# Attention loop of a polynomial-attention and expert block: units of two heads, fp32 scores, value products two key blocks behind, another reciprocal, the mask on the first square

## The chip, the cores and the metric

The kernel runs on one core of one Trainium2 chip. The metric is device time in microseconds of one execution, the median of several runs. Smaller is better.

The engines are named as in the profile: PE is TensorE (PEld its weight loads), DVE is VectorE, ACT is ScalarE, POOL is GpSimd, SP is the engine that issues DMAs.

## The reference

```python
x = L0_attn_x                                    # (4, 512, 512): 4 batches, 512 tokens, 512 features
x = x + attention(_layernorm(x))                 # 16 heads of 32
x = x + moe(_layernorm(x))                       # 16 experts, 4 per token, and a shared expert

# attention, for each batch and head
q, k, v = split(x @ w_qkv)                       # rotary position on q and k
q = layernorm_32(q) * ln_scale + ln_bias         # over the 32 features of a head; k the same
a = tril((q @ k.T) ** 4)                         # causal, fourth power instead of exp
out = (a / a.sum(-1)) @ v                        # then heads side by side, @ w_out
```

The expert part (router scores, choice of four experts, gate, up and down products) is the same before and after.

## The kernel before

One program of hand-written engine queues with semaphores. Its first part handles the four batches one after the other: `sequence(0, None)` is unrolled, batches 1 to 3 are a loop over the same body. The second part handles 96 tiles of 128 tokens through the shared expert and the chosen experts; the change does not touch it.

A batch has these stages:

1. **qkv, four blocks of 128 tokens.** PE multiplies (line 462), DVE applies the rotation and the norm of each head (lines 1159 to 1183), with one square on ACT between (line 746, released by line 1173, waited for by line 1177). PE transposes q and k (line 473), and ACT writes them with scale and bias: once as fp16 (line 712, the high half) and once as fp32 (line 716). DVE subtracts the two (`split_qk`, line 1149) and so gets the fp16 low half. The subtraction of block m-1 stands between lines 1173 and 1177 of block m.
2. **The attention loop.** Its 16 steps i are 4 groups of 4 heads (g) times 4 key blocks of 128 tokens (kb = i % 4). Because of the causal mask a step works on 512, 384, 256 and 128 query columns for kb 0 to 3, keys on the partitions. For each step PE makes the scores of 4 heads into 4 PSUM banks, each as three fp16 products (high-high, high-low, low-high; line 538). ACT squares each head from PSUM into `s_sq` (line 770). The second square goes into `s_p4`: heads 0 and 2 on DVE (line 1193), heads 1 and 3 on ACT (line 762). POOL multiplies the first 128 columns of each of the 4 heads by the causal mask (line 853). PE then makes the value product and, with a matrix of ones, the denominators (line 552), both accumulated over the key blocks of the group in banks 6 and 7. These products run one step behind the scores. `s_sq` has one buffer, `s_p4` has two, so the second square of step i waits for the products of step i-2.
3. **The end of a group.** `finish` on DVE takes the reciprocal of all 128x512 denominators (line 1141; a head's denominator stands on its 32 partitions alike) and multiplies (line 1143). The first value product of the next group (kb = 0) waits for it, since it starts banks 6 and 7 anew. `finish` of group g stands on DVE's queue after the second squares of step 4g+4, and for the last group after the loop.
4. **Beside the loop.** In every step ACT splits a piece of the expert weights into fp16 high part and rest (lines 682 and 684), and POOL makes the low part (line 861, `split_lo`), which is queued on POOL between the masks of one step and the next. In batches 1 to 3 DVE also does the routing of the batch before, a piece after the squares of most steps (`group_sums` in step 1 to `place_rows` in steps 9 to 12), and in all batches the statistics of the next batch's first norm in step 12 and its norm in step 14, which ACT follows with line 726.
5. **Output projection** (line 566), residual (line 1224), second norm, transposes.

The order on each engine is the order written in its function; nothing reorders it.

## Time and profile before

| | us |
|---|---|
| median of 3 runs (1252.7 to 1258.45) | 1253.88 |
| profiled execution, first to last instruction | 1278.8 |
| attention loop, batch 0 | 79 |
| attention loop, each of batches 1 to 3 | 95 |
| qkv stage of batch 1, with the transposes for the router | 54 |
| expert part, from 680 us on | 599 |

The profiled execution is known by its span alone; it is 24.9 us longer than the median of the runs without a profile. A row of the timeline has the start in us, the length in us (of one instruction, or from the first start to the last end of several), engine, line, operation, what is written and read, shape, and in brackets how long the engine had been idle and what ended that. A granted clock of 1.00 is TensorE at 2.4 GHz, 0.50 at 1.2 GHz.

### The profile page before, as it was taken

The numbers are of one execution on the slowest core, as the hardware profiler recorded it, in microseconds if no ns is written. First come the engines' busy times: TensorE is split into PE (matmuls) and PEld (weight loads), VectorE is DVE, ScalarE is ACT, GpSimd is POOL, SyncE is SP. The second block draws the span as 40 slices with busy tenths as digits, with TensorE's granted clock in tenths as the row PEclk, the third lists the DMA queues.
The fourth block names the chain that finished last, engine by engine and source line by source line (L and its number), as shares of the span: only waits on it lengthen the run. The fifth ranks groups of instructions, "written<-read, shape, count | busy, mean of one in ns | idle before, by whom it ended". The sixth has DMA issues, their size and how long they took to land. (4 is left out here: it accounts for less than half of the span.)

```text
span 1278.8 us, 21813 instructions
## 1 busy us (share of the span) xinstructions
PE 1013.0 (79%) x5786; PEld 483.4 (38%) x5787; DVE 782.5 (61%) x1641; ACT 571.1 (45%) x1018; POOL 503.3 (39%) x738
## 2 busy tenths in 40 slices
PE   5956799666997669976588889888888888878893
PEld 2422245222444214442145445344344344434341
DVE  2855578587695885858955866444544545544442
ACT  2377624767147672366735324333333333323330
POOL 0047500556003751026631102555555555555552
PEclk9977898677996689967787889999999999989997
DMA  8015430144501438104445786777877778877774
GB/s 323 1 50 188 159 131 1 50 149 146 183 3 49 140 107 327 69 0 148 148 149 178 264 321 216 188 171 178 187 185 179 170 177 191 192 154 183 169 178 77
DMA packets 76782, 194.36 MB, mean 152 GB/s; under 512 B 9920, under 2 KB 11072, under 8 KB 75328
## 3 DMA queue, kind: packets, MB, share of 16 engines
q1 hardware_dynamic: 58816, 150.58, 34.5%
q0 software_dynamic: 17920, 43.26, 18.9%
q8 instruction: 17, 0.28, 0.1%
q14 instruction: 29, 0.24, 0.1%
HBM read 132.72 MB, written 61.10 MB: 152 GB/s over the span
## 5 line engine op out<-in xcount | busy, mean ns | idle before, releaser
L606 PE MATMUL bank<-arena,xgT 128*128 (+1 forms) x1152 | 287.4, 387 | 4.0 <-ACT xgT L817 3.1
L853 POOL TENSOR_TENSOR s_p<-s_p,c_causal 128x128 f32<-128x128 f32 x256 | 128.8, 530 | 400.0 <-DVE s_p L1193 397.6
L552 PE MATMUL bank<-s_p,vtok 128*32 128x128 f32 (+3 forms) x512 | 118.0, 605 | 95.9 <-DVE arena L1143 49.5
L810 ACT ACTIVATE hT<-bank 128x512 f16<-128x512 f16 x96 | 57.3, 597 | 276.5 <-PE bank L616 264.6
L462 PE MATMUL bank<-arena 128*128 128x512 f32 x384 | 168.6, 597 | 2.0 <-issue 2.0
L606 PEld LDWEIGHTS bank<-arena,xgT 128*128 128x128 f16 x1152 | 109.6, 100 | 133.5 <-issue 44.4
L627 PE MATMUL bank<-wd,hT 128*128 128x512 f16 x576 | 152.7, 405 | 0.7 <-ACT hT L810 0.7
L898 POOL DMA_INDIRECT out<-yy,sidx x80 | 128.4, 1605 | 45.7 <-issue 44.7
L861 POOL TENSOR_TENSOR arena<-arena 128x768 f16<-128x768 f32 x68 | 115.7, 1702 | 71.9 <-ACT arena L684 71.5
L817 ACT ACTIVATE xgT<-bank 128x1024 f16<-128x1024 f16 x96 | 98.2, 1023 | 90.7 <-PE bank L597 89.1
L1367 DVE TENSOR_SCALAR yy<-bank,hsc 128x512 f32<-128x512 f32 x80 | 60.0, 750 | 125.8 <-DMA out<-yy,sidx 106.6
L1193 DVE TENSOR_TENSOR s_p<-arena 128x512 f32<-128x512 f32 (+3 forms) x128 | 82.8, 679 | 78.0 <-ACT arena L770 73.3
L770 ACT ACTIVATE arena<-bank 128x512 f32<-128x512 f32 (+3 forms) x256 | 97.8, 436 | 63.9 <-PE bank L538 37.4
L597 PE MATMUL bank<-ident,xg 128*128 128x128 f16 x768 | 62.7, 228 | 74.7 <-DMA xg<-xn_scratch,gidx 74.7
L462 PEld LDWEIGHTS bank<-arena 128*128 128x128 f32 x384 | 72.6, 192 | 89.9 <-issue 89.9
L892 POOL DMA_INDIRECT xg<-xn_scratch,gidx x80 | 85.0, 1063 | 41.3 <-issue 40.3
L1327 DVE TENSOR_TENSOR hh<-sg,bank 128x256 f32<-128x256 f32 x96 | 40.3, 419 | 90.3 <-ACT sg L826 85.7
L597 PEld LDWEIGHTS bank<-ident,xg 128*128 128x128 f16 x768 | 49.1, 102 | 112.4 <-DMA xg<-xn_scratch,gidx 103.4
L552 PEld LDWEIGHTS bank<-s_p,vtok 128*32 128x32 f32 x512 | 28.5, 121 | 153.3 <-POOL s_p L853 94.7
L552 PE MATMUL bank<-s_p,ones 128*32 128x128 f32 (+3 forms) x512 | 85.6, 578 | 0.0
L538 PE MATMUL bank<-arena 32*128 32x512 f16 (+3 forms) x768 | 61.5, 363 | 23.1 <-ACT arena L770 11.8
L627 PEld LDWEIGHTS bank<-wd,hT 128*128 128x128 f16 x576 | 55.4, 103 | 53.2 <-issue 11.3
(155 smaller groups left out, 1453.3 us busy)
## 6 DMA issues: line engine op xcount, KB each, us to landing
wd<-w_scratch SPq DMA_DIRECT2D x82, 512.0 KB
arena<-w_experts SPq DMA_DIRECT2D x34, 768.0 KB, 5.9
w_scratch<-arena SPq DMA_DIRECT2D x34, 768.0 KB, 4.5
arena<-w_scratch SPq DMA_DIRECT2D x17, 1024.0 KB, 8.0
xin<-x SPq DMA_DIRECT2D x5, 1024.0 KB, 9.1
arena<-x SPq DMA_DIRECT2D x4, 1024.0 KB, 7.1
x_scratch<-arena SPq DMA_DIRECT2D x4, 1024.0 KB, 4.5
xn_scratch<-vtok SPq DMA_DIRECT2D x4, 1024.0 KB, 5.0
```

Of the source, the lines that this page charges most:

```text
L462: mm = pe.matmul(bank[w][:], xnT[:, c, m * P:m * P + P], wqkv[:, c, w * E:w * E + E], start=(c == 0), stop=(c == EC - 1))
L552: mm = pe.matmul(bank[6 + n][r, P * kb:N], w, s_p4[:, (i - 1) % 2, j, 0:N - P * kb], start=(kb == 0), stop=(kb == MB - 1), skip_group_chec ...
L597: mm = pe.transpose(oct16(bank[k])[:, c], xg[:, k, 0:E].bitcast(F16)[:, c * P:c * P + P], ident16[:])
L606: mm = pe.matmul(bank[2 + k][:], xgT[:, k, xh * EC + c, :], w, start=(c == 0 and xh + wh == 0), stop=(c == EC - 1 and xh == 1))
L627: mm = pe.matmul(bank[5 + k][:], hT[:, k, hh_ * FC + c, :], wd[:, k, wh, c, :], start=(c == 0 and hh_ + wh == 0), stop=(c == FC - 1 and hh ...
L770: act.activation(s_sq[:, j, 0:N - P * kb], bank[j][:, 0:N - P * kb], ACT.Square, scale=1.0 / (QS * QS)).then_inc(sq_done, 1)
L817: act.activation(xgT[:, k], oct16(bank[k]), ACT.Copy).then_inc(gT_sb, 1)
L853: pool.tensor_tensor(d, d, C["causal"][:], ALU.mult).then_inc(p4_masked, 1)
L861: pool.tensor_tensor(halves[:, j, 1, a], stage[:, j, a], halves[:, j, 0, a], ALU.subtract).then_inc(lo_done, 1)
L892: pool.indirect_dma_start(out=xg[:, k], out_offset=None, in_=xn_dram, in_offset=bass.IndirectOffsetOnAxis(ap=gidx[:, k:k + 1], axis=0)).th ...
L898: pool.indirect_dma_start(out=out, out_offset=bass.IndirectOffsetOnAxis(ap=sidx[:, k:k + 1], axis=0), in_=yy[:, k], in_offset=None, comput ...
L1193: dve.tensor_tensor(s_p4[:, i % 2, j, 0:N - P * kb], s2, s2, ALU.mult).then_inc(p4_done[0], 1)
```

## The change

- q and k are written once, as fp32 (`qT`, `kT`); the fp16 halves, the factor of 64 and `split_qk` go. The scores of a head are one fp32 product in place of three fp16 products.
- A step has two units u of two heads each. ACT squares a unit in one instruction of 2 x w columns, from two PSUM banks. POOL masks the first 128 columns of both heads in one instruction, now in `s_sq`, between the two squares. DVE makes the second square of all units, one instruction each; ACT makes none.
- PE's value products run two steps behind the scores (`LAG = 2`).
- `finish` transposes the denominators in blocks of 32x32, takes the reciprocal of 16 columns in place of 512, and transposes them back, spread over 32 columns. It now stands after the squares of step 4g+5.

```diff
@@ PE
-                pe.wait_ge(qk_lo, b * (2 * MB) + 2 * MB)
+                pe.wait_ge(qkT_sb, b * (2 * MB) + 2 * MB)
-                for i in range(NG * MB + 1):
+                for i in range(UNITS // 2 + LAG):
...
-                        order = [(n, j) for n in range(3) for j in range(HG)]
-                        for n, j in order:
-                            if i and n == 0:
-                                pe.wait_ge(sq_done, b * (NG * MB * HG) + (HG * (i - 1) + j + 1))
...
-                            mm = pe.matmul(bank[j][:, 0:N - P * kb], k16[r, kh, g, P * kb:P * kb + P],
-                                           q16[r, qh, g, P * kb:N], start=(n == 0), stop=(n == 2))
+                        for u in (2 * i, 2 * i + 1):
+                            if u >= 2:
+                                pe.wait_ge(sq_done, b * UNITS + (u - 1))
...
+                            for j in (u % 2 * 2, u % 2 * 2 + 1):
+                                r = slice(D * j, D * j + D)
+                                mm = pe.matmul(bank[j][:, 0:N - P * kb], kT[r, g, P * kb:P * kb + P],
+                                               qT[r, g, P * kb:N], start=True, stop=True)
+                            mm.then_inc(scores_ps, 1)
...
+                                if n == 0 and j % 2 == 0:
+                                    pe.wait_ge(p4_done, b * UNITS + (2 * (i - LAG) + j // 2 + 1))
@@ ACT
+                for i in range(UNITS // 2):
                     w = N - P * (i % MB)
+                    for u in (2 * i, 2 * i + 1):
+                        j = u % 2 * 2
+                        act.wait_ge(scores_ps, b * UNITS + (u + 1))
+                        if u >= 2:
+                            act.wait_ge(p4_done, b * UNITS + (u - 1))
+                        act.activation(s_sq[:, j:j + 2, 0:w], wide(j)[:, :, 0:w], ACT.Square).then_inc(sq_done, 1)
@@ POOL
+                        pool.wait_ge(sq_done, b * UNITS + (u + 1))
+                        d = s_sq[:, j:j + 2, 0:P]
+                        pool.tensor_tensor(d, d, C["causal"][:].unsqueeze(1).to_broadcast([P, 2, P]),
+                                           ALU.mult).then_inc(sq_masked, 1)
@@ DVE
             def finish(b, g):
                 dve.wait_ge(pv_done, b * (NG * MB) + (g * MB + MB))
-                dve.reciprocal(rec, bank[7][:])
+                blocks = lambda a: a.rearrange("p (c i) -> p c i", i=D)
+                dve.transpose(den_t, bank[7][:])
+                dve.drain()
+                dve.reciprocal(inv[:], blocks(den_t)[:, :, 0])
+                dve.drain()
+                dve.transpose(blocks(rec), inv[:].unsqueeze(2).to_broadcast([P, N // D, D]))
                 dve.drain()
                 dve.tensor_tensor(attT[:, g, :], bank[6][:], rec, ALU.mult).then_inc(att_done, 1)
...
                     if i >= 2:
+                        dve.wait_ge(pv_done, b * (UNITS // 2) + (i - 1))
+                    for u in (2 * i, 2 * i + 1):
+                        j = u % 2 * 2
+                        dve.wait_ge(sq_masked, b * UNITS + (u + 1))
+                        s2 = s_sq[:, j:j + 2, 0:N - P * kb]
+                        dve.tensor_tensor(s_p4[:, i % 2, j:j + 2, 0:N - P * kb], s2, s2, ALU.mult).then_inc(p4_done, 1)
-                    if i and kb == 0:
+                    if i > MB and kb == 1:
                         finish(b, i // MB - 1)
```

## Rows read from the trace of the kernel before

**Rows 1.** The page's busy times, shares of the span and instruction counts.
```profile
PE 1013.0 (79%) x5786; PEld 483.4 (38%) x5787; DVE 782.5 (61%) x1641; ACT 571.1 (45%) x1018; POOL 503.3 (39%) x738
```
**Rows 2.** Stretches of time: length, busy time by engine, granted clock, DMA.
```profile
76.00:155.00 79.00, 57.76 (x455) 18.29 (x456) 46.37 (x51) 62.88 (x133) 57.83 (x80) 0.79 0.44 148
229.00:324.00 95.00, 64.67 (x506) 23.94 (x507) 72.15 (x130) 66.38 (x136) 58.85 (x80) 0.75 0.37 124
```
**Rows 3.** Timeline, batch 1, step 3 to 4, POOL and DVE.
```profile
248.93 4.17 POOL L853 TENSOR_TENSOR s_p<-s_p,c_causal 128x128 f32<-128x128 f32 x4 [1.31 <-DVE s_p L1193]
248.97 1.49 DVE L999 TENSOR_TENSOR rb<-mb 128x1024 f32<-128x1024 f32 x1
```
**Rows 4.** Timeline, batch 0, second group: the end of a group, until the next.
```profile
96.40 3.34 DVE L1141 RECIPROCAL qkn<-bank 128x512 f32<-128x512 f32 x1
99.82 0.69 DVE L1143 TENSOR_TENSOR arena<-bank,qkn 128x512 f32<-128x512 f32 x1
100.56 1.94 PE L552 MATMUL bank<-s_p,vtok 128*32 128x512 f32 x8 [4.50 <-DVE arena L1143]
114.72 3.35 DVE L1141 RECIPROCAL qkn<-bank 128x512 f32<-128x512 f32 x1
```
**Rows 5.** Stretches of the same: the stall of PE, and the products after it.
```profile
96.40:100.50 4.10, 0.00 (x0) 0.00 (x0) 4.03 (x4) 4.04 (x9) 3.23 (x5) 0.86 0.82 256
100.50:104.10 3.60, 3.54 (x16) 0.60 (x16) 0.94 (x3) 1.18 (x2) 3.04 (x5) 0.50 0.35 145
```
**Rows 6.** Timeline, batch 1: qkv stage, the square on ACT and what stands beside it.
```profile
193.61 1.28 DVE L1149 TENSOR_TENSOR arena<-s_p,arena 128x512 f16<-128x512 f32 x2
193.72 1.06 ACT L746 ACTIVATE arena<-arena 128x1024 f32<-128x1024 f32 x1 [1.16 <-DVE arena L1173]
```
**Rows 7.** Groups by line and shape: count, busy us, mean ns of one, idle before.
```profile
L716 ACT ACTIVATE s_p<-bank,ln_b,ln_s 128x512 f32<-128x512 f32 x32 | 25.1, 783 | 0.0
L817 ACT ACTIVATE xgT<-bank 128x1024 f16<-128x1024 f16 x96 | 98.2, 1023 | 90.7 <-PE bank L597 89.1
L770 ACT ACTIVATE arena<-bank 128x512 f32<-128x512 f32 x64 | 34.9, 599 | 26.9 <-PE bank L538 18.0 <-DVE s_p L1193 8.8
L770 ACT ACTIVATE arena<-bank 128x256 f32<-128x256 f32 x64 | 21.2, 385 | 26.6 <-DVE s_p L1193 13.6 <-PE bank L538 12.6
L684 ACT ACTIVATE arena<-arena 128x768 f32<-128x768 f32 x68 | 57.3, 843 | 2.1
L853 POOL TENSOR_TENSOR s_p<-s_p,c_causal 128x128 f32<-128x128 f32 x256 | 128.8, 530 | 400.0 <-DVE s_p L1193 397.6 <-ACT s_p L762 2.2
L1166 DVE TENSOR_TENSOR arena<-arena 128x1024 f32<-128x1024 f32 x16 | 19.6, 1225 | 1.5
L1179 DVE RECIPROCAL hs<-hs 128x32 f32<-128x32 f32 x16 | 5.6, 353 | 6.2 <-ACT hs L748 6.2
```
**Rows 8.** Timeline, batch 0 and 1: second squares, a mask, a low part.
```profile
78.32 0.69 DVE L1193 TENSOR_TENSOR s_p<-arena 128x512 f32<-128x512 f32 x1 [2.18 <-ACT arena L770]
79.17 0.45 POOL L853 TENSOR_TENSOR s_p<-s_p,c_causal 128x128 f32<-128x128 f32 x1 [76.47 <-DVE s_p L1193]
82.61 1.64 POOL L861 TENSOR_TENSOR arena<-arena 128x768 f16<-128x768 f32 x1 [1.15 <-ACT arena L684]
93.48 3.00 DVE L1193 TENSOR_TENSOR s_p<-arena 128x512 f32<-128x512 f32 x2 [1.15 <-ACT arena L770]
299.31 1.28 DVE L1193 TENSOR_TENSOR s_p<-arena 128x512 f32<-128x512 f32 x2
```
**Rows 9.** Timeline, scores of 512 columns, batch 0 and batch 1.
```profile
76.20 1.47 PE L538 MATMUL bank<-arena 32*128 32x512 f16 x12 [2.75 <-DVE arena L1149]
247.05 0.82 PE L538 MATMUL bank<-arena 32*128 32x512 f16 x12
```
**Rows 10.** Timeline, DVE, batch 1: the stretch with routing, and the end.
```profile
276.70 0.69 DVE L1193 TENSOR_TENSOR s_p<-arena 128x512 f32<-128x512 f32 x1 [3.66 <-ACT arena L770]
319.88 3.36 DVE L1141 RECIPROCAL qkn<-bank 128x512 f32<-128x512 f32 x1 [2.29 <-PE bank L552]
```

More of the change, by code:

```diff
@@ L61 @@
 CH = NCOL // P
+UNITS = NG * MB * 2
+LAG = 2
 NEG = 1.0e30
@@ L161, in build @@
         xnT = over([EC, N])
-        q16, k16 = (over([NG, N]).bitcast(F16).rearrange("p g (h n) -> p h g n", h=2) for _ in range(2))
+        qT, kT = (over([NG, N]) for _ in range(2))
         s_sq = over([HG, N])
@@ L206, in build @@
         hs = sa("hs", [P, 3, 2 * H])
[L207 removed]
+        den_t, rec = qkn[:, 0:N], qkn[:, N:2 * N]
+        inv = sa("inv", [P, N // D])
         xn16 = vtok[:].rearrange("p m e -> p (m e)").bitcast(F16).rearrange("p (m h e) -> p m h e", m=MB, h=2)
```

81 lines of the change are left out of this document (19 added, 62 removed).

## The prediction

> **What bounds the kernel now.** I read the page first, then the table of stretches, then the timeline engine by engine, and last the groups by line. No engine fills the span: PE is busy for 79% of it, DVE for 61% [rows 1]. So the stages are read apart. The change touches the attention loop, 79 us in batch 0 and 95 us in each later batch, 364 us in all, and the few us before and after it. In the loop PE has work for 57.76 of 79 us although it runs at its lower level for about half of it (mean clock 0.79 and 0.75). ACT is busy for 62.88 and POOL for 57.83 of the 79; DVE has 46.37 of 79 in batch 0 and 72.15 of 95 with routing [rows 2]. No engine is full, so what counts is which waits are in series. Three things show in the timeline.
>
> First, POOL and DVE shut each other out. Four masks that need 0.45 us each [rows 8] took 4.17 us while DVE ran its comparisons of two SBUF operands, and the comparison of 1024 columns took 1.49 us [rows 3] where an undisturbed operation of that size takes 1.22 us [rows 7]. They take turns.
>
> Second, the end of a group stalls PE. The reciprocal takes 3.34 us, the product 0.69 us, and PE has by then been idle for 4.50 us [rows 4]. In the 3.6 us after it the granted clock is 0.50, the 1.2 GHz level [rows 5]; the value products and the ones of 512 columns, sixteen instructions, fill 3.54 us of it [rows 5]; the last ends overlap, and I reckon 3.4 us for all, 1.7 for the values alone. From one reciprocal to the next a group of batch 0 takes 114.72 - 96.40 = 18.3 us [rows 4].
>
> Third, in batches 1 to 3 DVE is the pace from step 2 to step 12: squares, reciprocals and routing follow each other, with one hole of 3.66 us at step 8, where it waits for ACT [rows 10].
>
> **Prices.** A unit's square on ACT: 1.02 us for 1024 columns, 0.60 for 512, 0.39 for 256 [rows 7], 0.81 for 768 between them. The two splits of a step take 1.7 us together (0.84 each, [rows 7]). A second square of a unit on DVE: 1.22 us for 1024 columns [rows 7], 0.69 for 512 [rows 8], by the line through these 0.95 for 768 and 0.42 for 256. A mask over both heads: 128 columns take 0.45 and the 768 of the low part 1.64 us [rows 8]; by that line 256 columns take 0.69. Its ends are 0.45 (no more than one of today's) and 0.90 (two of them).
>
> The new `finish`: no transpose by DVE is in the trace. I take 0.69 us for each, as the 512-column operation beside it [rows 8]; the nearest ends are 0.35, what a reciprocal of 32 columns takes [rows 7], and 1.22, an operation of 1024. With 0.25 us for 16 reciprocals (below 0.35 for 32) and 0.69 for the product, and 0.1 for drains, that is 2.4 us against 4.1, 1.7 less (ends: 1.7 us and 3.5 us in all). The Trainium skill (Vector Engine (DVE) Microarchitecture Reference, 3.8 The reshape front-end and per-opcode configuration) says the transpose sustains one element per cycle per lane. By that the estimate for 512 columns is the same 0.69; no row here shows it.
>
> The scores: today twelve fp16 instructions on four row groups take 0.82 us at 2.4 GHz and 1.47 us at 1.2 GHz [rows 9]. An fp32 product is two instructions, and four heads of value products side by side take 1.7 us at the lower level, as above [rows 4, 5]. I give a pair of heads the same: 1.7 us at the lower level and 0.85 at the upper for 512 columns, so a step's two pairs in series take twice that (bound below: both pairs side by side, 0.85; above: no two heads side by side, 3.4 at the upper level). A group has 1280 columns, 2.5 times 512: at the lower level its products take 8.5 us, its scores 3.2 us today (less the ends in the 1.47) and 8.5 us then, so PE's work goes from 11.7 to 17.1 us.
>
> **What it removes before the loop.** Two of four qk writes on ACT (0.67 us each from start to start, mean 0.78 [rows 7]) and the last subtraction (0.64, half of 1.28 [rows 6]) go from the path from the last transposes to the first scores: 2.0 us a batch. The subtractions of blocks 0 to 2 bring nothing: they stand at 193.61 beside the square on ACT, 1.06 us from 193.72, which DVE has to wait for anyway [rows 6]. Where ACT is also late with copies for the router (batches 1 to 3), the writes saved let PE start 1.3 us earlier, of which 1.2 us remain. The first pair of scores at the lower level costs 1.70 against 1.47: +0.2.
>
> **A middle group in batch 0**, as I lay it out with these prices, zero at the first square of its first step (8, say). ACT squares 0 to 1.0 and 0.9 to 1.9, splits to 3.5. POOL has the low part of step 7 until 1.8, masks to 2.5 and 3.2. DVE's square runs to 4.2, the low part of step 8 takes its turn to 5.8, DVE's other square ends at 6.9. Step 9 is like it: squares from 4.3 and 6.9, DVE done at 10.0. Then `finish` to 12.3, the value products of step 8 to 15.8 (lower level) or 14.1 (upper). Only then may DVE square step 10 (its buffer is that of step 8), to 17.0; step 11 starts at 16.5 and step 12 at 18.7, plus 0.6 because its scores stand behind the products of step 9 on PE. So 19.3 us, 17.3 at the upper level, 21 if all of PE's work runs at the lower. Against 18.3: +1.0 for each of two groups. ACT loses 0.95 us of work a step and gains nothing by it, since the second squares on DVE and the masks between them are now the chain.
>
> The first group has no `finish` but the same chain: 15.9 us, against 93.48 - 78.32 = 15.2 us between the second squares of steps 0 and 4 [rows 8]: +0.7. From step 12 to the end: the norm statistics delay both alike; between -2.9 and +1.4, the end of the last group being 1.7 us shorter but the products of two steps behind it. I take +0.3 (a stall of the products of step 12, partly at the lower level). Batch 0: -2.0 + 0.2 + 0.7 + 2.0 + 0.3 = **+1.2 us**.
>
> **Batches 1 to 3.** Before the loop -2.0 - 1.2 + 0.2 = -3.0. In step 1 DVE's squares cost +1.7. In steps 2 to 11 DVE is the pace: its squares add 0.53 for each 512 columns it now does for ACT, 2.65 us for a whole group, so 0.5 + 0.3 + 2.65 + 2.65 = +6.1; two `finish` -3.3. The hole of 3.66 at step 8 becomes square 1.02, mask 0.69, hand-overs 0.2, less the square of the other unit 0.4: 1.5, so -2.1 (rounded). Two masks in place of four get in DVE's way less often, -1.2. The products that delayed DVE in batch 0 lie beside routing here (the expert weights after `finish` in step 5, the placing of rows after that in step 9). The end +0.3 as in batch 0, with its two `finish` in it. Sum -1.5 each, **-4.5 us** for three.
>
> **Sum.** +1.2 - 4.5 = -3.3 us. On the profiled execution, 1278.8, that gives 1275.5. It is 24.9 us above the median and the change has no part in that, so the difference is carried over: 1253.9 - 3.3 = 1250.6 us. A measurement of this kernel can tell about 0.5%, 6.3 us, from no change.
>
> The rule of the Trainium skill behind the first observation is in SBUF — State Buffer, SBUF: two separate sides: a DVE operation with two SBUF inputs and a GpSimd operation exclude each other for the whole instruction. The trace agrees (4.17 us). Without it the squares of DVE and the low parts of POOL would run side by side, and a middle group would take some 3 us less (two low parts of 1.64 leave the chain), which for batch 0 alone would be -6.
>
> **Rivals.**
> - *Slower: the mask in the chain.* DVE's square now waits for POOL, whose masks are queued behind the low part of the step before, and that behind ACT's split, which follows a square that waits for DVE. I let routing hide this in batches 1 to 3. For it speaks that POOL's masks already stretch to four times under routing [rows 3]; against it, that a piece of routing stands between the squares of most steps and gives the masks time. If DVE waits 0.5 us in each of steps 2 to 12 of three batches, that is +16.5: 1267. From 0.1 us a step on, the sign turns. Chance 0.20.
> - *Slower: PE at the lower level.* With 17.1 us of work in a group of 18 to 19, PE is the pace where it stays at 1.2 GHz. +2 in the first and +2.0 in two more groups of batch 0, +1.4 at each end, +1.5 in later batches: about +16, 1267. For: 0.50 right after the stall [rows 5]. Against: it has more to do, and the stall before the products shrinks from 4.5 to some 3 us. Chance 0.10.
> - *Slower: fp32 heads of different row groups don't overlap.* Scores of a 512-column step take 3.4 us; +1.5 a group in batch 0, +1 in others: about +18, 1269. For: order j, j of two passes each; against: the value products overlap fully [rows 4]. Chance 0.06.
> - *Faster: two steps of lag keep PE at 2.4 GHz.* Then a middle group of batch 0 takes 17.3 (-4.0 for two against my 19.3), the ends take 2 us less in each batch (-8), and the products of step 0, at the lower level today, free the start of the later loops (-2 in each of three): 1250.6 - 18 = 1233, or half of it, 1242. I put it at 1240. Chance 0.28.
> - *As laid out*: 1250.6, own range 1244 to 1258. Chance 0.36.
>
> **Range and chances.** The unknown prices weigh: `finish` up to 1.1 us dearer or 0.7 us cheaper at 16 places, +18 or -11; masks 0.2 either way at 128 units, of which about half are on the chain, 13 us. Not all go one way. The range is 1233 to 1270. Faster by over 0.5%: the faster rival 0.27 and 0.13 of my own case, 0.40. Slower: 0.16 + 0.09 + 0.05 and 0.02 of my own, 0.32. Within 0.5%: 0.28. My time lies within, but the cases around it hold more.
>
> **What would show it.** The qkv stage shorter by 2 to 3 us up to the first scores; the distance of two L1143-like products in batch 0 near 19 us; a `finish` of 2.4 us; DVE busy in the loop of batches 1 to 3 nearly all the time between steps 2 and 12; masks of 0.69 us; granted clock of the loops still near 0.8. I am wrong if a middle group of batch 0 is under 17 us or over 21, if DVE shows a wait for POOL in most steps with routing, or if PE's idle time in the loop is gone.

## The result: 4.6% slower

The changed kernel takes 1314.59 us (1309.39 to 1318.82, 4 runs) against 1256.16 us of the kernel before on the same chip (1252.7 to 1259.6, 4 runs): ratio 1.0458, 95% interval [1.0414, 1.0503]. I had forecast 1250.6 us, in a range of 1233 to 1270. The profiled execution has a span of 1315.3 us.

A yardstick used from here on is the length of an attention loop, from the first scores to the first product of the output projection, and ahead of it the time from the first qkv product to the first scores. Both are read from the timelines, in us:

| | qkv to scores, batch 0, 1, 2, 3 | loop, batch 0, 1, 2, 3 |
|---|---|---|
| before | 58.3, 61.0, 59.6, 60.6 | 74.2, 90.4, 89.0, 89.3 |
| after | 57.6, 57.7, 57.6, 57.6 | 85.1, 105.8, 105.8, 105.7 |

Before the loops the change gains 9.0 us in all; the loops lose 10.9 us in batch 0 and 16.2 us on average in each later one, 59.5 us in all. Together that is 50.5 of the 58.4 us between the two medians; where the other 8 us lie is not shown. The rest of an execution, from the last projection on, is mainly the expert part, which the change doesn't touch. It took between 608 and 628 us in the kernels below, without order (627.5 before, 612.5 after), and is not read further. So small differences are read from the loops and not from the ratios.

The page of the kernel after, its busy times (as [rows 1] of before):
```profile
PE 999.0 (76%) x5530; PEld 478.7 (36%) x5531; DVE 798.3 (61%) x1639; ACT 496.6 (38%) x730; POOL 508.5 (39%) x610
```
The table of stretches, first the loops of batch 0 and 1 after, then the same loops before. Columns: start and end, length, busy time and instructions of PE, PEld, DVE, ACT and POOL, granted clock, DMA share, GB/s.
```profile
75.40:160.50 85.10, 52.46 (x384) 17.69 (x384) 46.62 (x54) 49.58 (x69) 58.33 (x48) 0.70 0.38 130
235.20:341.00 105.80, 60.06 (x433) 23.01 (x433) 80.29 (x132) 52.85 (x73) 59.57 (x48) 0.66 0.31 105
```
```profile
76.20:150.40 74.20, 53.16 (x448) 16.26 (x448) 42.18 (x48) 62.88 (x133) 56.25 (x80) 0.80 0.44 149
229.40:319.80 90.40, 60.43 (x497) 21.93 (x497) 67.80 (x126) 66.38 (x136) 57.75 (x80) 0.74 0.36 123
```
The busy time of PE and of POOL is about the same, and ACT has 13 us less in each loop. In batch 1 DVE has 12.5 us more. In batch 0 it has only 4.4 us more, yet the loop is 10.9 us longer: more work in sum is not the whole reason there, but what stands behind what.

The timeline of DVE after, batch 0, steps 2 to 6, with the end of the first group. Columns as in [rows 4].
```profile
89.78 2.81 DVE L1176 TENSOR_TENSOR s_p<-arena 128x512 f32<-128x512 f32 x2 [2.67 <-PE bank L553]
93.28 1.22 DVE L1176 TENSOR_TENSOR s_p<-arena 128x256 f32<-128x256 f32 x2 [0.69 <-POOL arena L839]
97.19 4.24 DVE L1176 TENSOR_TENSOR s_p<-arena 128x1024 f32<-128x1024 f32 x2 [2.69 <-POOL arena L839]
102.12 0.96 DVE L1176 TENSOR_TENSOR s_p<-arena 128x768 f32<-128x768 f32 x1 [0.69 <-POOL arena L839]
...
104.57 0.71 DVE L1129 STREAM_TRANSPOSE qkn<-bank 128x512 f32<-128x512 f32 x1
105.36 0.25 DVE L1131 RECIPROCAL inv<-qkn 128x16 f32<-128x16 f32 x1
105.69 0.71 DVE L1133 STREAM_TRANSPOSE qkn<-inv 128x512 f32<-128x512 f32 x1
106.48 0.69 DVE L1135 TENSOR_TENSOR arena<-bank,qkn 128x512 f32<-128x512 f32 x1
110.93 1.29 DVE L1176 TENSOR_TENSOR s_p<-arena 128x512 f32<-128x512 f32 x2 [3.76 <-PE bank L553]
```
And what POOL does between the two squares of the step at 97.19:
```profile
98.19 2.16 POOL L848 TENSOR_TENSOR arena<-arena 128x768 f16<-128x768 f32 x1 [0.42 <-ACT arena L685]
```
Three things are to be seen that hold DVE up. It waits 0.6 to 0.7 us for a mask even where nothing else is in the way. Between the two squares of the step at 97.19 stands a low part of POOL: two squares of 1.22 us take 4.24. And at key block 2, the third step of each group, DVE waits for PE in batch 0 (2.67 us at step 2, 3.76 at step 6): a second square may be written only when the value products of two steps ago have been made, and these now stand on PE's queue behind the scores of the square's own step.

DVE's waits by releaser, loop of batch 1, after and then before (us in total, times, longest):
```profile
DVE s_p L1176 <- POOL arena L839: 20.6, 7, 9.0
DVE s_p L1176 <- PE bank L553: 4.7, 3, 3.9
```
```profile
DVE s_p L1193 <- ACT arena L770: 15.4, 6, 4.6
```
The longest of the 20.6 us, 9.0 before the first square, began 5.1 us before the loop's first scores, so 15.5 of them lie in the loop. By the table of stretches DVE is idle for 25.5 us of this loop after (105.80 - 80.29) and for 22.6 before: of the 15.4 us by which the loop of batch 1 grew, 12.5 are time in which DVE is busy, and only 2.9 are idle time.

The groups of the kernel after by line and shape, to be read against [rows 7]:
```profile
L839 POOL TENSOR_TENSOR arena<-arena,c_causal 128x256 f32<-128x256 f32 x128 | 119.0, 938 | 426.0 <-ACT arena L760 424.1
L848 POOL TENSOR_TENSOR arena<-arena 128x768 f16<-128x768 f32 x68 | 128.4, 1888 | 94.5 <-ACT arena L685 94.5
L1176 DVE TENSOR_TENSOR s_p<-arena 128x1024 f32<-128x1024 f32 x32 | 54.6, 1729 | 57.1 <-POOL arena L839 56.4 <-issue 0.7
```
A mask of both heads that nothing disturbs takes about 0.70 us, as forecast; its mean is 0.94. A square of 1024 columns takes 1.23 us undisturbed; its mean is 1.73. DVE and POOL still shut each other out, and now a mask that is late makes DVE late too.

The end of batch 1, DVE after:
```profile
321.97 2.46 DVE L956 BATCH_NORM_STATS2 st<-xin 128x6 f32<-128x512 f32 x4
324.51 0.38 DVE L960 BATCH_NORM_AGGREGATE mv<-st 128x2 f32<-128x6 f32 x4
324.80 1.81 DVE L1176 TENSOR_TENSOR s_p<-arena 128x768 f32<-128x768 f32 x2
326.53 0.71 DVE L1129 STREAM_TRANSPOSE qkn<-bank 128x512 f32<-128x512 f32 x1
...
328.43 0.69 DVE L1135 TENSOR_TENSOR arena<-bank,qkn 128x512 f32<-128x512 f32 x1
332.98 1.29 DVE L1176 TENSOR_TENSOR s_p<-arena 128x512 f32<-128x512 f32 x2 [3.85 <-PE bank L553]
```
The third `finish` now stands behind the placing of rows and the statistics of step 12 and the squares of step 13. Before, it stood ahead of the routing of its step (300.51, the statistics at 306.61). PE's products of two steps queue up behind it, and DVE then waits for them.

### The profile page after: what moved, and what is told of

Same layout as the page of the kernel before. It is cut to its first block and busy times, and to the rows that moved or that the text cites. A ratio compares the mean times of both kernels' runs of the same rounds, so it can differ in the third digit from the quotient of the medians.

```text
span 1315.3 us, 20485 instructions
## 1 busy us (share of the span) xinstructions
PE 999.0 (76%) x5530; PEld 478.7 (36%) x5531; DVE 798.3 (61%) x1639; ACT 496.6 (38%) x730; POOL 508.5 (39%) x610
## 3 DMA queue, kind: packets, MB, share of 16 engines
q0 software_dynamic: 17920, 43.26, 17.8%
## 5 line engine op out<-in xcount | busy, mean ns | idle before, releaser
L607 PE MATMUL scores<-arena,xgT 128*128 (+1 forms) x1152 | 284.1, 383 | 3.6 <-ACT xgT L803 3.1
L839 POOL TENSOR_TENSOR arena<-arena,c_causal 128x256 f32<-128x256 f32 x128 | 119.0, 938 | 426.0 <-ACT arena L760 424.1
L1176 DVE TENSOR_TENSOR s_p<-arena 128x1024 f32<-128x1024 f32 (+3 forms) x128 | 134.3, 1083 | 119.0 <-POOL arena L839 86.7
L465 PE MATMUL scores<-arena 128*128 128x512 f32 x384 | 169.3, 599 | 1.9 <-issue 1.9
L540 PE MATMUL scores<-arena 32*128 32x128 f32 (+3 forms) x512 | 111.4, 667 | 72.9 <-ACT arena L760 69.0
L607 PEld LDWEIGHTS scores<-arena,xgT 128*128 128x128 f16 x1152 | 108.1, 99 | 129.6 <-issue 39.7
L760 ACT ACTIVATE arena<-scores 128x1024 f32<-128x1024 f32 (+3 forms) x128 | 87.3, 701 | 150.1 <-DVE s_p L1176 131.9
L803 ACT ACTIVATE xgT<-scores 128x1024 f16<-128x1024 f16 x96 | 98.4, 1025 | 81.7 <-PE scores L598 79.2
L598 PE MATMUL scores<-ident,xg 128*128 128x128 f16 x768 | 60.7, 223 | 66.0 <-DMA xg<-xn_scratch,gidx 65.0
L465 PEld LDWEIGHTS scores<-arena 128*128 128x128 f32 x384 | 72.8, 192 | 90.3 <-issue 90.3
L866 POOL COPY wr<-xg 128x1 f32 x80 | 60.0, 750 | 13.9 <-PE scores L598 10.8
```

The lines of the kernel that those rows point to most:

```text
L465: mm = pe.matmul(bank[w][:], xnT[:, c, m * P:m * P + P], wqkv[:, c, w * E:w * E + E], start=(c == 0), stop=(c == EC - 1))
L540: mm = pe.matmul(bank[j][:, 0:N - P * kb], kT[r, g, P * kb:P * kb + P], qT[r, g, P * kb:N], start=True, stop=True)
L598: mm = pe.transpose(oct16(bank[k])[:, c], xg[:, k, 0:E].bitcast(F16)[:, c * P:c * P + P], ident16[:])
L607: mm = pe.matmul(bank[2 + k][:], xgT[:, k, xh * EC + c, :], w, start=(c == 0 and xh + wh == 0), stop=(c == EC - 1 and xh == 1))
L760: act.activation(s_sq[:, j:j + 2, 0:w], wide(j)[:, :, 0:w], ACT.Square).then_inc(sq_done, 1)
L803: act.activation(xgT[:, k], oct16(bank[k]), ACT.Copy).then_inc(gT_sb, 1)
```

## Experiments

Fifteen kernels. All ratios are to the kernel before, measured with it on one chip. Loops are batch 0 and the mean of batches 1 to 3.

| kernel | ratio, interval | loop, batch 0 | later |
|---|---|---|---|
| changed kernel | 1.0458 [1.0414, 1.0503] | 85.1 | 105.8 |
| a_mask_last | 1.0247 [1.0176, 1.0318] | 79.1 | 100.6 |
| a_mask_last_act | 1.0205 [1.0136, 1.0275] | 76.2 | 92.7 |
| a_lag1 | 1.0426 [1.0355, 1.0496] | 81.5 | 105.9 |
| a_low64 | 1.0030 [1.0000, 1.0060] | 79.5 | 92.6 |
| a_ml_act_lag1_pad | 0.9848 [0.9816, 0.9880] | 71.1 | 86.6 |
| b_fp32 | 1.0106 [1.0077, 1.0135] | 76.1 | 90.7 |
| b_fp32_pad | 0.9962 [0.9922, 1.0001] | 75.8 | 90.1 |
| b_fin | 0.9919 [0.9888, 0.9949] | 69.8 | 87.3 |
| b_fin_fp32 | 0.9877 [0.9829, 0.9924] | 72.3 | 88.2 |
| b_ff_lag2 | 1.0158 [1.0109, 1.0207] | 83.1 | 95.1 |
| b_low64 | 0.9752 [0.9717, 0.9787] | 71.2 | 81.0 |
| b_ff_lowdve | 0.9832 [0.9805, 0.9858] | 66.5 | 86.5 |
| d_unit_lag2_4buf | 0.9807 [0.9759, 0.9854] | 68.5 | 87.3 |
| d_unit_lowdve | 0.9747 [0.9696, 0.9798] | 64.8 | 84.5 |
| d_unit_lowdve1 | 0.9666 [0.9614, 0.9717] | 61.5 | 83.4 |

### Undoing parts of the changed kernel

**a_mask_last**: the mask back on the second square.
```diff
-                        pool.wait_ge(sq_done, b * UNITS + (u + 1))
-                        d = s_sq[:, j:j + 2, 0:P]
+                        pool.wait_ge(p4_done, b * UNITS + (u + 1))
+                        d = s_p4[:, i % 2, j:j + 2, 0:P]
```


> The changed kernel with one part undone: POOL masks the first 128 columns of the second square in s_p4 (both heads of a unit in one instruction), behind DVE, and the value products wait for the mask. Theory C (chain: first square, mask and second square follow each other through the one buffer s_sq, and the next first square waits for all three): the mask leaves the chain, 32 units a batch at 0.7 us and a hand-over, of which a half is not hidden by routing: 20 to 40 us less than the changed kernel, ratio to before 1.015 to 1.030. Theory D (DVE's doubled work and its mutual exclusion with POOL set the time): DVE and POOL do the same work, so no more than 8 us change, ratio 1.040 to 1.050. Theory P (fp32 scores and PE at its lower level): no change, ratio 1.046.

Loops 6.0 and 5.2 us shorter, 21.6 us in all: the mask in the chain is 2.1 of the 4.6%, less than half.

**a_mask_last_act**: in addition ACT makes the second square of the second unit, and DVE only that of the first (its part of the edit is not shown).
```diff
...
+                    act.activation(s_p4[:, i % 2, 2:4, 0:w], s_sq[:, 2:4, 0:w], ACT.Square).then_inc(p4_done[1], 1)
```


> As a_mask_last, and ACT makes the second square of the second unit of each step (2 heads at once), DVE only that of the first: the division of before, in units of two heads. Theory D: DVE is rid of 2.6 us a head group, 10 us a batch, and POOL meets it less often: 30 us or more less than a_mask_last, ratio at or under 1.01. Theory C: the chain still goes through one second square, the gain over a_mask_last is small, 0 to 10 us. Theory P: ratio 1.04 still, as the scores are the same.

Loops again 2.9 and 7.9 us shorter. The ratio hardly moved, though, because of something else: in batches 2 and 3 the time from the first qkv product to the first scores is 66.5 us in place of 57.6, 17.8 us in sum. That is taken up under b_fp32_pad.

**a_lag1**: value products one step behind, `finish` at key block 0.
```diff
-LAG = 2
+LAG = 1
-                    if i > MB and kb == 1:
+                    if i and kb == 0:
```


> The changed kernel with the value products one step behind the scores and finish after the squares of step 4g+4, both as before. If the lag is to blame (the end of a head group delays the second squares of two steps later, and the last products stand two steps behind): 10 us or more less than the changed kernel, ratio 1.03 to 1.038. If the lag was a gain that the rest hides: ratio above 1.05. Theories C and D: within 6 us of the changed kernel, ratio 1.041 to 1.051.

3.6 us in batch 0 and nothing in the later ones. I concluded that the lag was neutral. That was wrong, and the stretches of the loop show why: in the later batches the part from step 12 to the projection is 3.3 us shorter (23.7 for 27.0), and steps 4 to 8 are 4.1 us longer (29.4 for 25.3). Two effects cancel. In batch 0, DVE's wait for PE at step 2 stays (2.67 us in the changed kernel), so it is not the lag's doing:
```profile
90.83 1.73 DVE L1176 TENSOR_TENSOR s_p<-arena 128x512 f32<-128x512 f32 x2 [2.84 <-PE bank L553]
```

### One part alone

**b_fp32**: the kernel before with q, k and scores as in the change.
```diff
-                        order = [(n, j) for n in range(3) for j in range(HG)]
...
+                        for j in range(HG):
...
+                            mm = pe.matmul(bank[j][:, 0:N - P * kb], kT[r, g, P * kb:P * kb + P],
+                                           qT[r, g, P * kb:N], start=True, stop=True)
```


> The kernel before with one part of the change alone: q and k written once in fp32, no subtraction, one fp32 product a head. Theory P: the scores take up to twice as long on PE and hold back the first squares: ratio 1.01 to 1.03. Theories C and D: PE has room, and 2 us (batch 0) and 3.3 us (each later batch) before the loop are saved as the two traces show: ratio 0.990 to 0.995.

The loops are 1.9 and 1.1 us longer, and the time before the first scores should be shorter by 9 us in all, so the ratio must come from elsewhere. Where batch 1 reads 57.6 us before its first scores, batches 2 and 3 read 65.5 and 66.5. In the timeline DVE is idle right behind the turn of its loop over the batches and waits for nothing that the profile shows; PE then waits for DVE:
```profile
347.68 0.69 DVE L1143 TENSOR_TENSOR arena<-bank,c_rope_cos 128x512 f32<-128x512 f32 x1 [8.02 <-issue]
350.44 2.05 PE L460 MATMUL bank<-arena 128*128 128x512 f32 x2 [6.28 <-DVE arena L1147]
```

**b_fp32_pad**: the same, with 16 drains that have nothing to wait for.
```diff
+                for _ in range(16):
+                    dve.drain()
                 dve.wait_ge(xres_in, b * 16 + 16)
```


> The kernel before with fp32 q, k and scores, and 16 drains on DVE ahead of its wait for the residual, in every batch, where it has nothing else to do (+1 us of DVE time at most, beside PE's projection). DVE then runs 352 instructions from turn to turn in place of 336. Theory (the 8 us at the turn of the loop are instruction loading and depend on how the code lies): the stall goes, qkv to first scores in batches 2 and 3 is 57.6 in place of 66 us, the kernel is some 16 us faster than with fp32 scores alone, ratio to the kernel before 0.995 to 1.0. Rival (it comes from what fp32 scores change in the data or the queues): the stall stays, ratio 1.01.

The stall is gone; the first rotation of batch 2 comes 1.01 us after the instruction before it:
```profile
340.21 0.69 DVE L1143 TENSOR_TENSOR arena<-bank,c_rope_cos 128x512 f32<-128x512 f32 x1 [1.01 <-PE bank L460]
```
So added instructions made the kernel 1.4% faster (0.9962 for 1.0106), and fp32 scores as such are worth 0.4%, at the edge of what the interval can tell from nothing. The count of DVE's instructions from turn to turn is not the rule, though. With 336 and 320 DVE's idle time there is 8.0 to 8.6 us, with 337, 349, 350 and 352 about 1.0, and with 365 and 369 (b_fin, b_ff_lowdve) 1.6 to 3.0: a small stall.

**b_fin**: the kernel before with the new `finish` (its four operations as in the change), at its old place.
```diff
-                dve.reciprocal(rec, bank[7][:])
+                dve.transpose(den_t, bank[7][:])
...
+                dve.reciprocal(inv[:], blocks(den_t)[:, :, 0])
...
+                dve.transpose(blocks(rec), inv[:].unsqueeze(2).to_broadcast([P, N // D, D]))
```


> The kernel before with the new finish alone (transpose, reciprocal of 16 columns, transpose, product), at its old place (key block 0 of the next group). The finish takes 2.4 us in place of 4.1. In the kernel before, three of the four of a batch stand on the path of PE (its value products wait for them), the fourth beside the output projection. Theory (the gain is real, the loss of the change lies elsewhere): 12 x 1.65 = 20 us less, up to 25 where the shorter stall also keeps PE's clock; ratio 0.98 to 0.99. Rival (the stall is hidden by the second squares of the next step): ratio 0.995 to 1.0.

0.8% faster. The loops are 4.4 and 2.3 us shorter, 11 us in sum and not 20. Each `finish` is 1.5 us shorter (2.6 for 4.1). In batch 0 three of the four count (the stretches from step 4 to 8, from 8 to 12 and from 12 on are 1.9, 1.5 and 1.0 us shorter); the last one lies beside the projection, which starts before it ends. In later batches only half of what the three save reaches the end of the loop.

**b_fin_fp32**: both together.

> The kernel before with the new finish and with fp32 q, k and scores, nothing else. If the two add up: -20 from the finish, -12 before the loops, +3 to +6 in the loops, so 0.98 if DVE's turn of the loop does not stall, and 1.0 if it stalls as it did with fp32 scores alone (8 us before the first rotation of batches 2 and 3, +16). DVE runs 352 instructions from turn to turn here, as many as in the changed kernel, which did not stall; 336 and 320 stalled, 349 (the kernel before) did not. By the reading that the layout of DVE's code decides, no stall here.

0.9877, no stall. The two good parts of the change add up to some 1.2%.

### The lag

**b_ff_lag2**: b_fin_fp32 with the value products two steps behind and, as the lag needs it, `finish` one step later; nothing else of the change.
```diff
-                for i in range(NG * MB + 1):
+                for i in range(NG * MB + 2):
...
-                    if i:
-                        g, kb = divmod(i - 1, MB)
+                    if i >= 2:
+                        g, kb = divmod(i - 2, MB)
...
-                    if i and kb == 0:
+                    if i > MB and kb == 1:
```


> The kernel before with fp32 scores and the new finish, and now the value products two steps behind and the finish at key block 1. Against the same without the lag (loops 72.3 and 88.2 us, ratio 0.988). Theory (the lag is neutral, as in the changed kernel, where taking it back moved the loops by -3.6 and +0.3 us): within 2 us a loop, ratio 0.985 to 0.995. Rival (the lag costs where DVE is not the pace, since the second square waits for products queued behind the scores of the step): +3 us or more a loop, ratio 1.0. Other rival (PE keeps its clock): loops 3 us shorter, ratio 0.977.

The rival, and by far: loops 10.8 and 6.8 us longer, ratio 1.0158 for 0.9877. The loop of batch 0 in the table of stretches, b_fin_fp32 and then b_ff_lag2:
```profile
75.80:148.10 72.30, 59.34 (x385) 20.63 (x385) 37.75 (x54) 63.13 (x133) 56.16 (x80) 0.77 0.45 153
```
```profile
74.90:158.00 83.10, 68.64 (x385) 27.95 (x385) 33.31 (x54) 63.24 (x133) 55.18 (x80) 0.67 0.39 133
```
No engine has more instructions, and PE's clock is lower, not higher. What is new are waits of both squaring engines for PE's products in this stretch, which b_fin_fp32 does not have:
```profile
DVE s_p L1180 <- PE bank L549: 22.8, 6, 4.2
ACT s_p L755 <- PE bank L549: 16.5, 6, 4.2
```
**a_ml_act_lag1_pad**: the changed kernel without mask first, without DVE's extra squares and without the lag (32 drains against the stall); the units of two heads remain.

> The changed kernel with the mask back behind the second square, the second unit's second square back on ACT, the lag back to one, the finish back at key block 0, and 32 drains on DVE ahead of its wait for the residual (352 instructions from turn to turn). It differs from the kernel before with fp32 scores and new finish (loops 72.3 and 88.2) only in that squares and masks go in units of two heads. No stall at the turn of the loop: qkv to first scores 57.6 in all batches. Theory (a unit is a coarser pipeline: the second square starts only after 1.0 us of first square in place of 0.6, and the scores of the next step wait for a whole unit): loops 75 and 91, ratio 1.0. Rival (units cost nothing, fewer instructions): loops 72 and 88, ratio 0.988.

Against a_mask_last_act the loops are 5.1 and 6.2 us shorter: here the lag can be seen in the changed kernel too. And units beat single heads (b_fin_fp32) by 1.2 and 1.7 us (the rival of my expectation, and more): 0.9848, with an interval that overlaps that of b_fin_fp32.

**d_unit_lag2_4buf**: a_mask_last_act, so lag two, but with a buffer for each key block and the 32 drains (the 256 columns of key block 2 in a new tile, the 128 of key block 3 in the unused end of key block 1).
```diff
+        s_p4b = sa("s_p4b", [P, HG, N // 2])
+        p4 = lambda i, j, w: s_p4b[:, j, 0:w] if i % MB == 2 else (
+            s_p4[:, min(i % MB, 1), j, (N - P if i % MB == 3 else 0):(N - P if i % MB == 3 else 0) + w])
...
-                    if i >= 2:
-                        dve.wait_ge(pv_done, b * (UNITS // 2) + (i - 1))
+                    if i >= 4:
+                        dve.wait_ge(pv_done, b * (UNITS // 2) + (i - 3))
```


> The changed kernel with the mask behind the second square and the second unit's second square on ACT (both as before), the value products two steps behind and the finish at key block 1 as in the change, and a fourth-power buffer for each of the four key blocks in place of two, so that the second square of step i waits for the products of step i-4, not i-2. The same with two buffers took loops of 76.2 and 93.0 us, with lag one 71.1 and 86.8. Theory (two steps of lag cost because they were added without a buffer: the second square waits for products that stand behind the scores of its own step): loops 71 and 87 or less, ratio 0.985 or below. Rival (the lag itself costs, as finish and the end come later): loops stay at 75 and 92, ratio 1.005.

68.5 and 87.3 us where two buffers took 76.2 and 92.7. The lag was dear because it came without a buffer: in the loop of batch 0 the kernel with two buffers has the wait below, and with four no second square waits for PE.
```profile
DVE s_p L1179 <- PE bank L554: 14.3, 4, 3.8
```
DVE's timeline in batch 0 with four: the square of step 6 starts right behind `finish`, where the changed kernel waited 3.76 us for PE (110.93 above).
```profile
100.65 0.69 DVE L1143 TENSOR_TENSOR arena<-bank,qkn 128x512 f32<-128x512 f32 x1
101.25 1.21 DVE L1182 TENSOR_TENSOR s_p4b<-arena 128x512 f32<-128x512 f32 x1
```
With buffers, lag two is 2.6 us better than lag one in batch 0 and 0.7 worse in later ones; the ratios, 0.9807 and 0.9848, have intervals that overlap.

### POOL's low part

**a_low64** and **b_low64**: the low part of the expert weights cut from 768 to 64 columns, in the changed kernel and in the kernel before.
```diff
+                if not (isinstance(b, int) and b == 0 and i < 4):
+                    a = slice(q * PIECE, q * PIECE + 64)
```


> The changed kernel with POOL's low part of the expert weights cut from 768 to 64 columns from the fifth piece on (the rest of the low parts is left out); a low part then takes 0.3 us in place of 1.9. Theory D/exclusion (the loops are longer because DVE's doubled squares and the mask before them take turns with POOL): the low part sits between the masks of one step and the next and each turn costs DVE up to its length, so the loops of batch 0 lose 8 us or more and those of batches 1 to 3 4 to 8 us each, ratio to the kernel before 1.01 to 1.02. Rival (plain serial work of DVE: 1.22 us per square where half of it was on ACT, exclusion matters little): loops shorter by 2 us at most, ratio 1.04.

> The control for the changed kernel with the low part of the expert weights cut to 64 columns: the same cut in the kernel before (the rest of the low parts is left out). If the exclusion of DVE and POOL is what the change made dear, the cut brings the kernel before much less than the 46 us it brought the changed one: loops shorter by 2 to 4 us a batch, ratio 0.99. Rival (the low parts cost both kernels the same, and the change lost its time elsewhere): loops shorter by 6 us in batch 0 and 13 in each later batch as in the changed one, ratio 0.965.

The cut takes 5.6 and 13.2 us from the loops of the changed kernel, 45 us in all, but also 3.0 and 8.6 us, 29 us in all, from those of the kernel before. Neither theory holds whole: the low parts were already dear, and the change made them dearer by 16 of its 59.5 us. That it is mostly the exclusion shows in DVE's busy time, with the same instructions on DVE: in the loop of batch 1 it falls from 80.29 to 65.19 us (kernel before: 67.80 to 57.46), by more than the loop itself. The part that comes from masks which no longer queue behind a low part was not tested apart. The groups by shape of a_low64, then of b_low64:
```profile
L1178 DVE TENSOR_TENSOR s_p<-arena 128x1024 f32<-128x1024 f32 x32 | 41.9, 1326 | 57.9 <-POOL arena L839 57.2 <-issue 0.7
L850 POOL TENSOR_TENSOR arena<-arena 128x64 f16<-128x64 f32 x64 | 34.6, 541 | 99.0 <-ACT arena L685 99.0
```
```profile
L1195 DVE TENSOR_TENSOR s_p<-arena 128x512 f32<-128x512 f32 x32 | 25.1, 801 | 30.1 <-ACT arena L770 29.4 <-issue 0.7
```
DVE's squares of 1024 columns fall from 1729 to 1326 ns in the changed kernel, those of 512 from 888 to 801 ns in the kernel before.

**b_ff_lowdve**: b_fin_fp32 with the low part on DVE, at the end of each step.
```diff
-                    split_lo(b, i)          # POOL
...
+                dve.tensor_tensor(halves[:, j, 1, a], stage[:, j, a], halves[:, j, 0, a], ALU.subtract
+                                   ).then_inc(lo_done, 1)
```


> The kernel before with fp32 scores and the new finish, and the low part of the expert weights on DVE at the end of each step in place of POOL between the masks. On POOL it takes 1.64 us undisturbed and shuts DVE out meanwhile; on DVE an operation of 768 columns takes about 0.95 us and keeps the masks from nothing but itself. Theory of the exclusion: each step gives DVE back 0.7 us where it is the pace, and the masks no longer stand behind the low part: loops shorter by 4 us in batches 1 to 3, and by 0 to 4 in batch 0; ratio 0.975. Rival (DVE now waits for ACT's splits and its own queue is longer): loops 2 to 4 us longer, ratio 1.0. DVE's count from turn to turn is 368 to 384 here, so the stall of 8 us may come back in batches 2 and 3 (+16, to be read apart in the time before the first scores).

Loops 5.8 and 1.7 us shorter. More in batch 0 and less in later ones than I expected; the intervals of 0.9832 and 0.9877 overlap. The stall at the turn is small (369 instructions): the time before the scores is 58.4 and 59.1 us in batches 2 and 3. The loop of batch 1 in the table of stretches, b_fin_fp32 and then b_ff_lowdve:
```profile
221.90:310.20 88.30, 66.75 (x432) 25.55 (x432) 65.64 (x132) 66.52 (x137) 58.05 (x80) 0.79 0.37 125
```
```profile
215.40:302.00 86.60, 66.48 (x433) 26.16 (x433) 65.55 (x148) 66.46 (x137) 36.46 (x64) 0.74 0.38 128
```
DVE has 16 instructions more and is busy for as long as without them.

**d_unit_lowdve**: the same move in a_ml_act_lag1_pad, without the 32 drains.

> Units of two heads, fp32 scores, new finish, lag one, mask behind the second square, ACT's half of the second squares (loops 71.1 and 86.8, ratio 0.985), and the low part of the expert weights on DVE. With single heads that move brought 5.8 us in batch 0 and 1.2 to 2.2 in each later batch. If it adds up: loops 66 and 85, ratio 0.980. Rival (the units had already taken the gain by fewer masks): loops 70 and 87, ratio 0.985. DVE runs 352 instructions or so from turn to turn; should it stall at the turn, the time before the scores of batches 2 and 3 shows it.

It adds up: 64.8 and 84.5 us, 0.9747.

**d_unit_lowdve1**: DVE scales as it subtracts, ACT's second split goes.
```diff
-                dve.tensor_tensor(halves[:, j, 1, a], stage[:, j, a], halves[:, j, 0, a], ALU.subtract
+                dve.scalar_tensor_tensor(out=halves[:, j, 1, a], in0=stage[:, j, a], scalar=WS, in1=halves[:, j, 0, a],
+                                         op0=ALU.mult, op1=ALU.subtract).then_inc(lo_done, 1)
```


> The same with DVE scaling the weights as it subtracts (one operation in place of ACT's second split of 0.84 us and DVE's subtraction), so ACT has one split a step. ACT's 64 second splits are 54 us of its time in the loops. Where ACT's next first square waits behind the splits (batch 0) loops get 3 to 8 us shorter against the one above, in later batches 0 to 3; ratio 0.970 to 0.978. Rival (ACT's splits are hidden behind PE's scores): no difference.

1227.03 us (1222.47 to 1229.59) against 1267.46 us of the kernel before beside it: 0.9666 [0.9614, 0.9717], 3.3% faster than before and the fastest of these kernels. Its loops are 3.3 and 1.1 us shorter than those of d_unit_lowdve; the intervals of the two ratios overlap. Its loops in the table of stretches:
```profile
74.80:136.30 61.50, 47.41 (x384) 15.91 (x384) 42.42 (x54) 46.84 (x69) 27.94 (x32) 0.83 0.53 180
210.20:293.80 83.60, 57.88 (x432) 20.66 (x432) 64.97 (x132) 50.05 (x73) 27.49 (x32) 0.76 0.39 133
```
DVE now does what POOL did and is still busy for 2.8 us less in batch 1 than in the kernel before (64.97 for 67.80); but the three new `finish` give 5.0 us of that (7.1 for 12.1). The move alone, from a_ml_act_lag1_pad to d_unit_lowdve, adds 3.8 us to DVE's busy time (61.66 to 65.47), for 16 operations that fill 16.7 us. POOL has 30 us less.

## Why the prediction was wrong

The parts, each undone on top of the one above it, read from the loops (batch 0, mean of later batches). They sum to the whole by construction (to rounding), so the sum is no test of them; their order matters, as a_lag1 and b_ff_lag2 show. The row of the lag holds the place of `finish` too.

| from, to | what | us |
|---|---|---|
| changed, a_mask_last | mask in the chain | +6.0, +5.2 |
| a_mask_last, a_mask_last_act | all second squares on DVE | +2.9, +7.9 |
| a_mask_last_act, a_ml_act_lag1_pad | second step of lag, two buffers | +5.1, +6.2 |
| a_ml_act_lag1_pad, b_fin_fp32 | units of two heads | -1.2, -1.7 |
| b_fin_fp32, b_fp32_pad | new `finish` | -3.5, -1.9 |
| b_fp32_pad, before | fp32 scores | +1.6, +0.6 |
| sum | | +10.9, +16.2 |

I had forecast -3.3 us for the whole and 58.4 were measured, 61.7 us more. By the terms below, 7.9 us of the miss lie in the loop of batch 0 (10.9 for 3.0), 14.7 in each later loop (16.2 for 1.5) and 1.8 ahead of the loops: 54 in all. Steps 0 to 12 of batch 2 in the table of stretches, before and then after:
```profile
398.00:464.40 66.40, 46.62 (x364) 16.78 (x364) 54.45 (x98) 50.52 (x105) 44.97 (x60) 0.73 0.35 119
```
```profile
420.10:494.90 74.80, 44.03 (x296) 16.25 (x292) 62.60 (x102) 38.11 (x53) 46.58 (x37) 0.66 0.35 117
```
Point by point, by the steps of the prediction; distances are between DVE's first squares of a step unless named otherwise.

- **Before the loop: right.** -3.0 forecast for batches 1 to 3; -3.3, -2.0 and -3.0 measured; -0.7 for -1.8 in batch 0.
- **Prices: right.** `finish` from 104.57 to 107.17, 2.6 us for 2.4; a mask 0.70 for 0.69; squares of 1.23 and 0.96 for 1.22 and 0.95, where nothing disturbs them. Heads in fp32 do overlap, the rival on that is out: the scores of four heads, 512 columns, take 2.09 us at the lower level when they run side by side (at 75.4), where 3.4 were forecast; a pair alone takes 1.13 at the upper level for 0.85. The loops with fp32 scores are longer by 1.6 and 0.6 us. The rival of PE as the pace at its lower level is not what happened either: the clock of the loop did fall, but PE's busy time in it did not grow (52.46 us for 53.16 and 60.06 for 60.43).
- **Middle groups of batch 0: right**, +1.1 and +1.3 us (19.6 us from step 4 to 8 and from 8 to 12) for +1.0 each. The hand layout had the mask, the low part between the two squares and the products behind `finish` in it, and all three stand in the trace where it has them.
- **The start: failed.** I laid groups out from their first square on and gave what lies ahead of it nothing. From the first scores to DVE's first square it is 4.1 us, 2.1 before: with fp32 scores alone it is 2.7, with units too 3.2 (one wide square in place of a head's), and the mask adds the rest. +2.0 in each of four batches.
- **First group of batch 0: failed**, +2.5 for +0.7. I had the wait for the products of two steps ago only behind `finish`; it also holds at step 2, where DVE waits 2.67 us. The lag doesn't make this wait (a_lag1 has it too, and a first group of 17.9 us); with the mask out of the chain the group takes 13.9 in place of 17.7.
- **The end: failed**, the largest miss, 22 us in all: from step 12 to the first projection +3.9 for +0.3, and +6.5 in later batches. I counted the last `finish` as 1.7 us shorter, but PE starts its projection 4.2 us before that `finish` ends (2.7 after), so its length is hardly in the loop. And `finish` of the third group, moved by one step, got behind the statistics. They "delay both alike" holds for the squares of step 13; only in the new kernel do `finish`, the products behind it and the squares of step 14 come after them as well. With lag and `finish` put back (a_lag1) the end is 2.4 us shorter in batch 0 and 3.3 in later ones. In later ones the placing of rows was stretched besides: its operations from step 12 on take 6.8 us in batch 2, 3.1 before.
- **Batches 1 to 3, steps 0 to 12: failed**, 20 us in all. My terms come to +1.2 us; it is +7.8 (mean). DVE is the pace, as I had it, but its time was mis-sized. On the mean of the three batches its squares grew by 11.4 us and not by the 7.8 of the undisturbed prices: I priced them as if POOL stood still, and POOL's operations shut DVE out. The two `finish` gave 3.4 (3.3 forecast). Masks "get in DVE's way less often, -1.2" gave nothing: what else DVE does there takes 32.2 us for 32.1. And DVE's idle time fell by 0.3 and not by 2.1: at step 8, where I let 1.5 us remain, it waits 3.4 and 0.6 us for masks. That products lie beside routing held at steps 6 and 10 (waits of 0.5 and 0.4 us) and not at step 14 (3.85 us at 332.98).
- **The rival that came nearest** is the mask in the chain, at 0.20 and 1267 us. It is real (a_mask_last) but it is 6.0 of 10.9 us in batch 0 and 5.2 of 16.2 in the later ones. It doesn't work as I wrote it, by 0.5 us of waiting in each of steps 2 to 12: in batch 1 DVE waits for a mask at steps 0, 1, 8 and 15, and 0.2 us at step 7. What spoke for it I misread: four masks in 4.17 us are 2.3 times their undisturbed 1.8, not four times. I had rivals one by one at 16 to 18 us each and never two at once; by the table above three parts of the change cost over 20 us each: the mask 21.6, all second squares on DVE 26.6, the lag 23.7. The rival of 0.28, that the lag keeps PE at 2.4 GHz, is refuted: the granted clock of the loop fell from 0.80 to 0.70 and, with the lag alone, from 0.77 to 0.67.
- **None of my three signs of being wrong came.** The middle groups are 19.6 us, DVE waits for POOL in few of the steps with routing, and PE still stands idle in the loop. I had set the signs where my layout was right, and none on the start, the end or the length of DVE's squares.
- **The rule on the two sides of SBUF** (the Trainium skill, SBUF — State Buffer, SBUF: two separate sides) holds here: with the low part cut, squares of 1024 columns go from 1729 to 1326 ns. I used it to price one group of batch 0 and not for the squares of batches 1 to 3.

What stays open: the price of the lag in the changed kernel itself depends on the order in which parts are undone (0 to 6 us a batch in the later ones), and the table gives one order.

## What to carry to other kernels

When products are moved a step further back, count the buffers that they read: the writer of the buffer now waits for work queued one step later, and here, without another buffer, the lag cost more than it hid. Forecast a loop from its first instruction to the first one of the next stage, not from one steady step to another, and when several edits lengthen the same chain, price them together. Where two engines shut each other out, don't price their operations undisturbed. An undo in the whole changed kernel can hide a part's cost: a_lag1 gained 3.3 us at one place of each later loop and lost 4.1 at another, where the lag alone costs 2.8%.

## What the runs showed of the hardware

- An engine's loop over a long body can stall at its turn. Two kernels lost 8 us there on DVE in each of batches 2 and 3, with instruction packets of 8192 bytes on queue q14 in those microseconds; 16 drains added to one of them took the stall away and made it 1.4% faster. The kernel before has such packets at its turn too (at 341.1 and 343.3 us) without a stall. So instructions that do nothing can decide it; by what rule, and whether the packets are the cause, was not found.
- Work taken from POOL and given to DVE cost DVE little or nothing: its busy time in batch 1 went from 65.64 to 65.55 us in one pair of kernels and from 61.66 to 65.47 in another, for 16 operations of 768 columns that fill 16.7 us. Of two engines that shut each other out, the faster one should have the work: one operation takes 1.04 us on DVE (mean) and 1.64 on POOL undisturbed.
- Operations on DVE with a single tensor input are stretched too. A scalar operation of 128 columns in fp16 takes 0.27 us alone and took 1.67 us in the changed kernel, until a low part of POOL that had begun before it was done at 317.85.
```profile
314.29 3.56 POOL L848 TENSOR_TENSOR arena<-arena 128x768 f16<-128x768 f32 x1 [0.88 <-ACT arena L685]
```
```profile
316.27 1.67 DVE L1102 TENSOR_SCALAR ra<-c_iota,kf 128x128 f16<-128x128 f32 x1
...
320.94 0.27 DVE L1102 TENSOR_SCALAR ra<-c_iota,kf 128x128 f16<-128x128 f32 x1
```
